# The decays of a unit's first chunk, made on ScalarE one step earlier, ahead of the Silu rows

## What is computed

```python
zxbcdt = u @ Wi.T                       # z, xBC, dt
xBC = silu(conv(xBC) + conv_b)          # -> x, Bm, Cm
dt = softplus(dt + dt_bias); A = -exp(A_log)
def step(h, inp):
    dA = exp(dt_t * A)
    h = h * dA + (dt_t * x_t) * B_t
    y_t = einsum('bhpn,bn->bhp', h, C_t)
y = (ys + D * x) * silu(z)
y = y * rsqrt(mean(y * y) + 1e-05) * norm_w
return y @ Wo.T
out = (out_f + reversed out_b) * 0.5
```

## Time and profile before

| | us |
|---|---|
| median of 3 runs | 852.98 |
| lowest, highest | 852.75, 858.59 |
| profiled execution, device time | 853.98 |
| its span, first to last instruction | 852.2 |
| ScalarE busy in it | 543.8 |
| VectorE busy in it | 496.4 |
| TensorE busy in it | 716.2 |
| ACT_TABLE_LOADs on the Exp of the scan (L2131) | 8 of 1.283 |

### The profile page before, as it was taken

One profiled execution on the slowest core, in us unless ns is written; L12 is line 12 of the kernel. 1 busy time (PEld: TensorE's weight loads), 2 busy tenths in 40 slices (PEclk: granted clock), 3 DMA queues, 4 the chain that ended last, 5 costly groups with the idle time before them and its releaser, 6 DMA issues. The chain is left out here.

```text
span 852.2 us, 12981 instructions
## 1 busy us (share of the span) xinstructions
PE 716.2 (84%) x4016; PEld 373.4 (44%) x4016; DVE 496.4 (58%) x1453; ACT 543.8 (64%) x938; POOL 298.8 (35%) x328
## 2 busy tenths in 40 slices
PE   4799999989999997898779886778887768797995
PEld 1432222212222224565446454566566645564654
DVE  6778432204855747743437469798798847332352
ACT  5367997889998983644256684967877615342331
POOL 3090003301000434434323456444562732545342
PEclk9799999999999999999889988998999979998998
DMA  4046934521492211112212042112221311211313
GB/s 130 1 187 161 183 86 81 199 91 60 175 261 82 86 36 50 40 34 50 80 28 55 20 117 56 58 50 60 71 72 52 99 49 56 58 42 47 88 53 89
DMA packets 76410, 70.11 MB, mean 82 GB/s; under 512 B 9687, under 2 KB 60233, under 8 KB 76080
## 3 DMA queue, kind: packets, MB, share of 16 engines
q1 hardware_dynamic: 71024, 60.56, 26.6%
q0 software_dynamic: 5024, 8.54, 3.0%
q10 hardware_dynamic: 288, 0.10, 0.1%
HBM read 41.23 MB, written 29.02 MB: 82 GB/s over the span
## 5 line engine op out<-in xcount | busy, mean ns | idle before, releaser
L687 ACT ACTIVATE attn_p<-attn_ps 128x1024 f32<-128x1024 f32 x256 | 240.7, 1059 | 34.7 <-PE attn_ps L703 20.7
L1665 PE MATMUL ps_main<-moe_xsT,moe_w 128*128 128x320 f32 x384 | 131.0, 469 | 14.6 <-issue 9.1
L703 PE MATMUL attn_ps<-attn_p,attn_v 128*32 128x512 f32 x1024 | 137.5, 608 | 4.2 <-issue 4.0
L1675 ACT ACTIVATE moe_act_h<-ps_main 128x320 f32<-128x320 f32 (+1 forms) x128 | 55.1, 433 | 115.2 <-PE ps_main L1665 60.6
L1690 DVE TENSOR_TENSOR moe_hid<-moe_act_h,ps_main 128x320 f32<-128x320 f32 (+1 forms) x128 | 61.9, 485 | 110.8 <-ACT moe_act_h L1675 51.0
L1559 POOL DMA_INDIRECT moe_slots<-rows,moe_scatter_at x64 | 63.8, 997 | 97.8 <-DVE moe_scatter_at L1548 38.0
L680 PE MATMUL attn_ps<-attn_q_rows,attn_k_rows 64*128 64x512 bf16 x448 | 84.5, 388 | 11.5 <-ACT attn_p L687 7.7
L1665 PEld LDWEIGHTS ps_main<-moe_xsT,moe_w 128*128 128x128 f32 x384 | 70.7, 200 | 49.7 <-issue 29.5
L1695 PE MATMUL ps_main<-moe_hid,moe_w 128*128 128x320 f32 (+1 forms) x256 | 74.9, 458 | 5.1 <-DVE moe_hid L1690 3.7
L680 PEld LDWEIGHTS attn_ps<-attn_q_rows,attn_k_rows 64*128 64x128 bf16 x448 | 20.3, 93 | 134.2 <-ACT attn_p L687 119.6
L1765 POOL DMA_INDIRECT moe_rows<-moe_y,moe_dest x48 | 46.2, 962 | 78.6 <-ACT moe_y L1758 39.7
(11 more groups left out here) (273 smaller groups left out, 1288.0 us busy)
## 6 DMA issues: line engine op xcount, KB each, us to landing
mb_cums<-mb_cum_kept SPq DMA_DIRECT2D x32, 256.0 KB
moe_slots<-zeros SPq DMA_DIRECT2D x4, 1380.0 KB, 14.0
attn_q_rows<-attn_q_parts SPq DMA_DIRECT2D x36, 128.0 KB
attn_k_rows<-attn_k_parts SPq DMA_DIRECT2D x36, 128.0 KB
moe_w<-in_w SPq DMA_DIRECT2D x3, 1536.0 KB, 11.6
moe_rows<-zeros SPq DMA_DIRECT2D x4, 1024.0 KB, 16.2
moe_back<-moe_rows SPq DMA_DIRECT2D x16, 256.0 KB, 4.0
mb_e_cum<-mb_e_cum_kept SPq DMA_DIRECT2D x56, 64.0 KB
```

The costliest lines, as they stand in the source:

```text
L687: self.core.nc.scalar.activation(self.p[:, w % self.PB, :, :].rearrange("p a n -> p (a n)"), self.ps_s[:, w % self.SB, :, :].rearrange("p ...
L703: ins = self.core.nc.tensor.matmul(self.ps_av[32 * i:32 * i + 32, :], self.v[:, b * TPB + kt, HGROUPS * i + m, :], self.p[:, w % self.PB, ...
L1665: self.core.nc.tensor.matmul(ps[:, w % 2, 0:CAP], wt[:, e, c * P:(c + 1) * P], self.xsT[:, u % 2, :], start=True, stop=True).then_inc(self ...
L1675: self.core.nc.scalar.activation(self.act_h[into, w % 2, :], self.ps_h1[rows, w % 2, 0:CAP], ACT.Silu).then_inc(self.silu_done, 1)
```

## The change

`exps` is split into three helpers: `lower` (the four Relus), `keep_b` (the copy of B) and `exp_lowered` (the Exp). For a chunk that is a unit's first (g = 8, 16, 24) `exps` now does only `keep_b`. Its Relus and its Exp are issued a step earlier: at i = 6 of the unit before, after `exps` of the last chunk and ahead of the gates. Everything else, the other 29 chunks among it, is issued as before, and no semaphore or buffer is new.

```diff
+    def exps(self, act, g):
+        ahead = g >= self.NC and g % self.NC == 0
+        if not ahead:
+            self.lower(act, g)
+        self.keep_b(act, g)
+        if not ahead:
+            self.exp_lowered(act, g)
...
         for hh in range(NH):
             ins = nc.scalar.activation(self.e_seg[:, g % 2, hh, :], self.cums[:, g % 2, hh, :], ACT.Relu, bias=self.cum[:, di, n, hh:hh + 1], scale=-1.0)
         ins.then_inc(self.lowered, 1)
+
+    def keep_b(self, act, g):
         act.wait_ge(self.b_done, g + 1)
         if g >= 2:
             act.wait_ge(self.st_done, self.passed(g - 2))
-        nc.scalar.copy(self.bs[:, g % 2, :], self.ps_b[:, 0:P]).then_inc(self.b_read, 1)
+        self.core.nc.scalar.copy(self.bs[:, g % 2, :], self.ps_b[:, 0:P]).then_inc(self.b_read, 1)
+
+    def exp_lowered(self, act, g):
         act.wait_ge(self.lowered, g + 1)
-        nc.scalar.activation(self.e_seg[:, g % 2, :, :], self.e_seg[:, g % 2, :, :], ACT.Exp, scale=-1.0).then_inc(self.seg_exp, 1)
+        self.core.nc.scalar.activation(self.e_seg[:, g % 2, :, :], self.e_seg[:, g % 2, :, :], ACT.Exp, scale=-1.0).then_inc(self.seg_exp, 1)
...
                     if g + 1 < N:
                         mamba.exps(act, g + 1)
+                    if u + 1 < UNITS and i == NC - 2:
+                        mamba.lower(act, g + 2)
+                        mamba.exp_lowered(act, g + 2)
```

More of the change, by code:

```diff
@@ L2115, in exps, with lower @@
     def exps(self, act, g):
+        ahead = g >= self.NC and g % self.NC == 0
[4 more added lines that the diff above has]
+            self.exp_lowered(act, g)
+    def lower(self, act, g):
         nc = self.core.nc
```

## The result

The changed kernel takes 864.15 us (median of 20 runs, 856.14 to 873.0), the kernel before 855.7 in the runs beside it (median of 20). The ratio is 1.0075, with a 95% interval of 1.0049 to 1.0102: some 6.4 us more (4.2 to 8.7), where 6.15 had been forecast. The ratio leaves out the slow executions, more than 1.5% above the fastest of their own kernel (5 of the changed kernel's 20), which the medians include; the medians alone would give 1.0099. On the 852.98 us that the forecast started from, the ratio gives 859.4. The profiled execution took 860.29 us against 853.98, with a span of 858.5 against 852.2.

A forecast was written before the change was run, and what follows sets the result against it. ScalarE's own program was taken to set the time across boundaries, VectorE inside the units. Terms 3.2 + 0.35 + 2.6 = 6.15 us on 852.98 gave 859.1 us, range 853.5 to 863.5.

The forecast's parts named there:

- the chance of most weight, within 1%: Whole kernel: time between 844.5 and 861.5 us, not told from no change by a measurement; chance 0.73.
- That VectorE's wait is not the bound: Across a boundary ScalarE's own program sets the time; VectorE's 3.06 us wait only moves to the next wait.
- The first rival: Boundaries 1 and 2: VectorE's waits of 3.06 and 3.19 us come out whole, giving 846.7 us; chance 0.08.
- The slip of 1.87 us: Ahead of the gates: Exp to table load takes 2.52 us instead of 0.65, so Silu rows start 1.87 later.
- Boundary 1, +3.2: Unit 1 to 2: ScalarE idles for TensorE's `turn`, then the load is uncovered; Exp(9) and first tap 3.2 us later.
- its second rival: The rival listed as a wash, with the later start finding TensorE's full clock; chance 0.20.
- Boundary 2, +0.35: Exp(17) comes 0.65 us later behind the copy of B, 0.29 is regained at `back`; net +0.35.
- The third rival: TensorE's clock falls (1.7 us boundary 2, 0.6 boundary 3) and `cums` is late (1.1): +3.4, 862.5 us; chance 0.19.
- Boundary 3, +2.6: Square root, normalising and `turn` come 1.87 us later, then the uncovered load; Exp(25) at 651.97 against 649.38.
- The dearer table switch: Fourth rival: boundaries 1 and 3 each pay 1.35 us more for the uncovered table load, 861.8 us; chance 0.03.
- Rows later by 1.9: Sign of being right: the Silu rows start 1.9 us later after the Exp of the last chunk.
- Eight loads on the Exp's line: Sign of being right: the number of table loads on L2131's Exp stays at eight, as before.

The follow-up runs named there:

- kernel with the slip alone: Kernel before, plus a second set of Relus and Exp of each next unit's first chunk ahead of the gates, old ones kept; 1.0048.
- boundary 1 alone: Changed kernel with only chunk 8's Relus and Exp issued ahead, chunks 16 and 24 as in the kernel before; 1.0011 to the kernel before.
- kernel with TensorE kept busy: Changed kernel plus five unread 128x384 matmuls per boundary in TensorE's idle time; 1.0057 to the kernel before.
- the faster kernel here: Kernel before with last chunks' copy of B behind Silu rows, chunk 7's Relus between square roots, last `z` row ahead of fourth Silu row; 0.9963.
- kernel with boundary 2 alone: Changed kernel with only chunk 16's Relus and Exp issued ahead, chunks 8 and 24 as in the kernel before; 0.9971 to the kernel before.

## Why the prediction was right, and where it was not

**The time and the direction: right.** +6.15 us forecast, +6.4 measured (4.2 to 8.7). The range and the chance of most weight, within 1%, hold it too. How near it came is in part luck: the second set of runs of the same kernel gave +12.6 (9.4 to 15.9), twice the forecast.

**That VectorE's wait is not the bound: right.** Its wait of 3.06 for the first chunk is gone, one of 2.87 stands at the second chunk in its place, and the time rose. The first rival needed the 6.25 us of two waits to come out whole; none of it did.

**The slip of 1.87 us: right.** It measures 1.83 at boundaries 1 and 3 and has the same length, within 0.05, in every kernel that puts the decays ahead and doesn't wait for `cums`. The kernel with the slip alone shows that it reaches the taps whole; that kernel costs 4.0 us (1.3 to 6.8).

**Boundary 1, +3.2: the mechanism right, the size by the state of the clock.** ScalarE idles ahead of the norm copy, released by TensorE, and the table load comes behind it, as the prediction wrote. It assumed that the clock would fall as in the earlier trace rows, and said in its second rival what would happen if the later start found the full clock. Both happened: +3.92 in one profile of the changed kernel, +1.67 in the other, and +1.67 also with boundary 1 alone and with `cums` sent early. The stretches of the four profiles are 52.60, 55.14, 52.60 and 52.61. So at the tap the cheaper case is the common one, and the term was too large by 1.5 us in most of them. What the prediction left out makes up for it further on: the lower clock at chunk 10, in all four, from which VectorE waits 2.6 us for TensorE in place of 1.0 (1.0, 1.0 and 2.1 in the three profiles with boundary 1 as before). Up to the Exp of chunk 15 boundary 1 costs 2.2, 4.4, 3.2 and 3.2 us in these four profiles, against the kernel before.

**Boundary 2, +0.35: the step that failed.** It measures +3.24. The prediction took the value of its lower bound for the wait for `cums`, as a lone send was held nearer to it; the send went out at 590.13 and the Relus that read it began at 593.43, so it took 3.3 us to be of use, and the wait was 1.27, in the upper half of the bounds 0 to 2.2. About 1.0 of it is no matter of the landing: the prediction took from the earlier trace rows that the send goes out 2.36 us ahead of the last Exp, and it went out 1.39 ahead. And the prediction left TensorE's clock at full. The third rival had both parts right at this boundary, 1.1 for the wait (1.27 measured) and 1.7 for the clock (14.85 - 13.31 = 1.54). Its reason for the clock, that the idle time grows with the slip, is borne out as far as the profiles go: with the slip alone TensorE idles 1.86 us more and the clock is 0.66. What this rival put on boundary 3 for the clock, 0.6, isn't there: Exp to Exp is 18.53 with the window behind the gates at 0.66 and 18.52 with it at 1.00. Without the wait and the lower clock the kernel with TensorE kept busy gives 0.42.

**Boundary 3, +2.6: right.** +2.53 in three profiles and +2.78 in the one with `cums` sent early, and the third stretch longer by 1.9 to 2.5 us. The root is later by the slip, VectorE's wait for it is 2.84, and the load behind the norm copies is out of its cover.

**The sum was right partly because two errors met.** 3.2 + 0.35 + 2.6 stands against 1.67 + 3.24 + 2.53 in the first profile. One term was 1.5 too high and one 2.9 too low. Measured without gaps between the terms it is 2.21 + 3.36 + 2.46 = 8.03: boundary 1 costs 1.0 less than forecast, boundary 2 3.0 more. The first error is a clock that was read in one execution of the kernel before and taken as a property of the place, where it differs between executions; half of the second is a clock read in the old order and carried over to the new one, which lowers it; the other half is the wait for `cums`.

**The dearer table switch: not there.** The load takes 1.28 us and the next instruction starts 1.30 after it began, in front of the gates (538.15 to 539.45) and in front of the Exp (550.24 to 551.53), also where nothing else covers it. The Trainium skill (ScalarE: Activation LUTs, "What ACT_TABLE_LOAD costs") counts a drain of 1380 ns on top. No trace here shows one, so the measurement decides.

**Signs to look for.** Rows later by 1.9: yes. No wait of `mt` at chunks 8 and 16 and one of about 3 at 9: yes, 2.87; at 25 it is 1.74, smaller, as VectorE itself was late by the root. Eight loads on the Exp's line: yes. ScalarE idle about 3 us at boundary 1: 3.23 or 1.40. First tap of unit 2 later by some 3: 3.92 or 1.67. The one sign named as wrong that did show is the wait for `cums` at chunk 16.

## What to carry to other kernels

A wait on one engine is a gain only if the engine it waits for has idle time before it; where that engine works without a gap, moving an instruction forward on it moves everything behind it back by the same length, and the wait turns up at the next consumer. Before moving work away from behind a block, ask what it covered: here a table load and four Relus filled the time in which another engine got ready. The cover also hid a lower clock of TensorE: 0.66 at boundary 2 cost nothing with it and about 1.5 us without it. Look for the opposite move, as the faster kernel here did: take out of the front of a full stretch what waits for somebody else and has a late reader.

## What the hardware showed that was not expected

- **The granted clock at one place of one program differs between executions.** In the 5 us around the `turn` of boundary 1 it was 1.00 and 0.50 in two profiles of the changed kernel, and with it four matmuls of L2225 took 0.69 or 1.20 us and the whole boundary 17.80 or 20.05. A clock read from one profile is a sample. The Trainium skill (TensorE: Matmul & The Clock Gate, "Part 1: The HAM clock gate (the "warmup" mystery)") says of a kernel's start that the moment at which the clock rises differs from run to run of one kernel. These traces show such a difference in the middle of one.
- **A change on ScalarE lowered TensorE's clock.** At boundary 2 it is 0.66 or 0.50 in all six profiles with the slip and TensorE not filled, each with a new idle time of 1.5 to 2.3 us ahead of the `z` projection, and 1.00 in the three without the slip.
- **Five unread matmuls in the idle time kept the clock at 1.00 at all three boundaries**, but gained only where another engine waited for TensorE: 1.54 us at boundary 2 of the changed kernel, nothing in the kernel before.
- **A lone send of 256 KB was of use 3.3 us after it was issued** (590.13 to 593.43), with nothing else issued by SyncE before 592.47; 3.31 with TensorE kept busy, and 3.00 in the changed kernel's second profile. In the kernel with boundary 2 alone it was issued at 587.82, and the Relus began at 591.12, again 3.3 later, with no wait shown: the landing took no longer than that.
